# A fused recommender kernel: pair multiplies re-divided between DMA and TensorE, half of the DMAs issued by ScalarE, and folds put ahead of gathers

## The chip, the cores and the metric

One core of a Trainium2 chip. The metric is the device time of one execution in microseconds (us); lower is better. Engines are called PE (TensorE), DVE (VectorE), ACT (ScalarE), POOL (GpSimd) and SP (SyncE, which here only issues DMAs).

## The reference, cut to what matters

For 2048 examples, 26 fields of 32 numbers each are looked up in tables (`emb`). Two interaction layers ("CIN") and a dense network of three layers are computed from them and summed with a linear part.

```python
emb = tables[feat_idx, sparse]              # (2048, 26, 32)
x0 = xk = emb
for w, bb in ((conv1_w, conv1_b), (conv2_w, conv2_b)):
    hp = einsum('bhd,bmd->bhmd', xk, x0).reshape(-1, h * M, E)
    xn = sigmoid(einsum('oi,bid->bod', w, hp) + bb[None, :, None])
    xk, rest = xn[:, :half], xn[:, half:]    # rest is summed over E
deep = tanh(tanh(tanh(deep_x @ W1 + b1) @ W2 + b2) @ W3 + b3) @ deep_w
```

The second layer's product pairs the first layer's 64 results with each of the 26 fields. It is the bulk of the work, and the change is about it.

## The kernel before, in words

The 2048 examples are 16 tiles of 128, and each tile is four steps (`STEPS`) of 8 of the 32 numbers, so that a step has 8 x 128 = 1024 columns. After the 64 steps the dense network runs over all examples; the change does not touch it.

In a step the 26 fields are 13 pairs (n = 0 to 12, which fields by `ORDER`). For pair n, DVE multiplies a 128 x 1024 tile, in which each of two fields is repeated on 64 partitions, with `xk` (line 545), and PE contracts the product into `y2` (`contract`, line 627, four matmuls a pair). The repeated tile comes in one of two ways:

- for n in `BY_DMA` (nine pairs) SP reads it from `x0_rows`, a copy of the tile's embeddings in HBM, by two broadcast DMAs of 256 KB each, one for either half (`spread_by_dma`, line 377), into a buffer `xb` of its own. DVE multiplies in place, so the buffer is free for the next step when PE has contracted that pair.
- for n in `BY_PE` (6, 7, 11, 12) PE spreads it with four small matmuls for two pairs (`spread_pair`, line 603) into one of three PSUM slots `bc`; DVE reads PSUM and writes `hp`.

The first layer of the next step is computed beside this: PE fills three slots (uses K, line 614), ACT squares them (line 793), PE contracts them in two column halves (`contract_k`, line 621, "first 0" and "first 1") into the one PSUM bank `xn`, and ACT reads each half by three activations (`read_xn`, lines 797 to 799). PE waits for the read of the first half before it starts the second. Use T turns the embeddings for a later step (line 590) and ACT copies them (line 783). Use D, once a tile at the end of step 2, turns the next tile's embeddings for the dense network (line 599); ACT copies them to `deep_t` (lines 787, 789), and SP writes them to `x0_rows` (`dump`).

The order of PE's and ACT's work in a step is written out in `STEP_WORK`; each slot use takes the slot of the use three places before it (`slot_free`). Each engine runs its own list in order.

POOL gathers the embeddings of the next tile by 26 indirect DMAs (`gather`, line 432). It may begin when D has been turned (`free_emb`, line 459). Between gathers, in the places that `AHEAD` sets, it folds the sums of both layers (`add_up`, lines 447 to 452). When all 26 have landed, ACT makes the high part of the embeddings (`make_high`, line 780, in step 1 of a tile, right after its copy of T) and POOL the low part (line 439).

ACT may read the first layer's results for a new tile into `r1` (in step 3) only when POOL's last `r1` fold is done.

Of the kernel before, what the change touches and what calls it, by code (L numbers as in the profile page):

```python
# [14 lines left out]
P = 128  # L15
B, M, V, D, ND = 2048, 26, 1250, 32, 13
ROW = D + 1
# [6 lines left out]
H = 64  # L24
# [64 lines left out]
def is_t(use):  # L89
    return isinstance(use, tuple) and use[0] == "T"  # L90


# [27 lines left out]

AHEAD = 4, 10, 16
assert AHEAD[-1] <= M

# [13 lines left out]
def build(nc, table, sparse, dense_t, lin_dense, pair_a, pair_b, diag_a, diag_b, w2rows, conv1_b, conv2_b,  # L137
          cin_w, scalars, W1, b1, W2, b2, W3, b3, deep_w, select, ident_f, out):
    with ExitStack() as ctx:
# [95 lines left out]
        pool_held = sem("pool_held")  # L235
        sp_held = sem("sp_held")
        gathered = sem("gathered")
        high_made = sem("high_made")
# [51 lines left out]
        def product(n):  # L290
            return hp[BY_PE.index(n)] if n in BY_PE else xb[BY_DMA.index(n)]

        GATHERED = 16 * M
# [39 lines left out]
        def _(sp):  # L333
# [32 lines left out]
            def dump(t):  # L366
                sp.wait_ge(deep_copied, t + 1)
                hold()
                cols = bass.ds(t * P, P)
                sp.dma_start(x0_rows[bass.ds(t, 1), 0:(KD - 1) * P, :].rearrange("t (k p) b -> p (t k) b", p=P),  # L370
                             deep_t[:, 0:KD - 1, cols]).then_inc(dumped, 16)
                sp.dma_start(x0_rows[bass.ds(t, 1), (KD - 1) * P:M * ROW, :].rearrange("t p b -> p (t b)"),
                             deep_t[0:LAST_E, KD - 1, cols]).then_inc(dumped, 16)
                sp.wait_ge(dumped, t * (16 * DUMPS) + 16 * DUMPS)
                hold()

            def spread_by_dma(t, sl, i):
                for f in range(2):
                    first = (2 * ORDER[BY_DMA[i]] + f) * ROW + sl * STEP_D
                    row = x0_rows[bass.ds(t, 1), first:first + STEP_D, :].rearrange("t d b -> t (d b)")  # L380
                    sp.dma_start(xb[i][H * f:H * f + H, :], row.to_broadcast([H, COLS])).then_inc(spread[i], 16)

            def tile(t, is_first, ahead):
                for sl in range(STEPS):
                    s = t * STEPS + sl
                    for i, n in enumerate(BY_DMA):
                        if not (is_first and sl == 0):
                            sp.wait_ge(contracted, contracted_by(s - 1, n))
                            hold()
                        spread_by_dma(t, sl, i)  # L390
                if ahead > 0:
# [24 lines left out]
        def _(pool):  # L416
# [48 lines left out]
            free_emb(0, 3)  # L465
            gather(range(AHEAD[2]))

            def tile(t, is_first, ahead):
                if ahead > 0:
                    gather(range(AHEAD[2], M - 4))  # L470
                if not is_first:
# [113 lines left out]
        def _(pe):  # L585
# [8 lines left out]

            def turn_deep(slot):
                rows = emb[:, 0:M, :].rearrange("p m e -> p (m e)")
                for k in range(KD):
                    n = min(P, M * ROW - k * P)
                    last = nc.tensor.transpose(bc[slot][0:n, k * P:(k + 1) * P], rows[:, k * P:k * P + n], idf[:, :])  # L599
                last.then_inc(filled, 1)  # L600
# [31 lines left out]
            def slot_free(t, sl, use, is_first, ahead):  # L632
# [12 lines left out]
                else:  # L645
                    pe.wait_ge(deep_copied, t + 2)

            def fill(t, sl, use, ahead):
# [12 lines left out]
                else:  # L661
                    turn_deep(slot)

# [3 lines left out]
            turn_x0(1, 1)  # L667
            turn_deep(2)
            for k in range(K1):
                pe.wait_ge(x0t_copied, min(k + 1, 2))  # L670
                if k == 2:
                    pe.wait_ge(deep_copied, 1)
                spread_sum(k, k, x0t[0])
# [8 lines left out]
            def tile(t, is_first, ahead):  # L682
                for sl in range(STEPS):
# [30 lines left out]
                    if ("D", 0) in there:  # L714
                        slot_free(t, sl, ("D", 0), is_first, ahead)
                        fill(t, sl, ("D", 0), ahead)

# [49 lines left out]
        def _(act):  # L767
# [16 lines left out]

            def copy_deep(slot, t):
                cols = bass.ds(t * P, P)
                nc.scalar.activation(deep_t[:, 0:KD - 1, cols], bc[slot][:, 0:(KD - 1) * P].rearrange("p (k b) -> p k b", b=P),
                                     ACT.Copy)
                nc.scalar.activation(deep_t[0:LAST_E, KD - 1, cols], bc[slot][0:LAST_E, (KD - 1) * P:KD * P],
                                     ACT.Copy).then_inc(deep_copied, 1)  # L790
# [10 lines left out]
            def read_y2(s, sl):  # L801
                act.wait_ge(contracted, s * PAIRS + PAIRS)
                nc.scalar.activation(r2[:, sl, :], y2[:, :], ACT.Sigmoid, bias=bias2[:, :]).then_inc(y2_read, 1)  # L803

            act.wait_ge(pads_cleared, 2)
            make_high(0)
# [5 lines left out]
            act.wait_ge(w1_step, 7)  # L812
            copy_deep(2, 0)
            for k in range(K1):
                act.wait_ge(filled, 3 + k + 1)
                square(k, k)
            for c in range(2):
                act.wait_ge(k_contracted, c + 1)
                read_xn(0, 0, c)
            act.wait_ge(w2_loaded, W2_LOADED)  # L820

            def tile(t, is_first, ahead):
                for sl in range(STEPS):
# [3 lines left out]
                    for kind, what in STEP_WORK:  # L827
# [11 lines left out]
                        elif kind == "of_last" and not start:  # L839
                            if sl == 1 and not is_first:  # L840
                                act.wait_ge(r2_step, t * SUMS)
                            read_y2(s - 1, (sl - 1) % STEPS)
                        elif kind == "first" and ("K", 0) in there:
                            act.wait_ge(k_contracted, k_contracted_by(s, what))
                            if what == 0:
                                act.wait_ge(multiplied, s * PAIRS + 1)
                                if sl == STEPS - 1:
                                    act.wait_ge(r1_step, (t + 1) * SUMS)
                            read_xn((sl + 1) % 2, (sl + 1) % STEPS, what)
                    if ("D", 0) in there:  # L850
                        act.wait_ge(filled, filled_by(t, sl, ("D", 0), ahead))
                        copy_deep(slot_of(sl, ("D", 0), ahead), t + 1)

# [108 lines left out]
```

## Time and profile before

| | us |
|---|---|
| median of three runs | 1829.8 (1819.85 to 1834.06) |
| the profiled execution | 1826.01 |
| its span, first to last instruction | 1824.2 |
| start, up to the first contraction of pairs | about 79 |
| one tile (four steps), mean of 14, from D turned at 129.98 to D turned at 1433.43 | 93.1 |
| dense network and end, from about 1538 | 286 |

The page gives busy shares over the span of 87% for PE, 63% for DVE, 39% for ACT, 43% for POOL. The SP and ACT queues' DMAs share 16 DMA engines. Because the tiles repeat, one is best read by the order of events in it: a gain per tile counts 14 times.

### The profile page before, as it was taken

The page shows a single profiled execution, that of the slowest core. Times are in us where ns is not written, and L with a number is a line of the kernel's source. Part 1 is how long each engine was busy: PE and PEld are TensorE (multiplying, and loading weights), DVE is VectorE, ACT ScalarE, POOL GpSimd, SP SyncE. Part 2 cuts the span into 40 slices and gives each one's busy share as a digit, 9 for nine tenths or more (in the row PEclk, how much of TensorE's full clock was granted, in tenths as well). Part 3 has the DMA queues.
Part 4 walks back from the last instruction along what each step waited for, and adds up shares of the span by engine and source line. Part 5 has one row for each costly group of instructions (what it writes and reads, how often), then busy time and mean ns, then how long its engine had stood idle before and what let it go on. Part 6 is the DMA issues. An engine that isn't in the chain of part 4 may idle for free.

```text
span 1824.2 us, 23564 instructions
## 1 busy us (share of the span) xinstructions
PE 1586.2 (87%) x6584; PEld 690.7 (38%) x6584; DVE 1154.8 (63%) x992; ACT 704.1 (39%) x966; POOL 784.1 (43%) x631
## 2 busy tenths in 40 slices
PE   0799889969998979698989798899897997999998
PEld 0333333323333323233323232333232332887886
DVE  2376777656867766568676677677766777344442
ACT  1343434333343434234434343344343432445443
POOL 6728282637382735454545554455555112000000
PEclk9899999989999989898989898999998998999999
DMA  4799999979999989899999999899998996223231
GB/s 85 167 235 209 223 211 228 214 176 212 231 219 213 220 192 214 182 208 225 209 219 210 215 215 218 204 214 218 230 216 203 215 235 157 88 92 99 92 98 47
DMA packets 132283, 344.73 MB, mean 189 GB/s; under 512 B 30131, under 2 KB 50899, under 8 KB 132183
## 3 DMA queue, kind: packets, MB, share of 16 engines
q1 hardware_dynamic: 118936, 337.23, 79.1%
q0 software_dynamic: 13312, 7.06, 3.1%
q8 instruction: 19, 0.31, 0.1%
q14 instruction: 16, 0.13, 0.0%
HBM read 337.14 MB, written 7.04 MB: 189 GB/s over the span
## 4 chain that ended last, share of the span: by engine, by line
PE 44%; POOL 29%; issue 13%; DMA 9%; ACT 3%; DVE 1%; POOLq 0%; SPq 0%; ACTq 0%; DVEq 0%
POOL emb L432 23%; PE y L627 16%; PE bc L740 14%; PE xn L621 10%; DMA emb<-table,idx_stage 7%; POOL r L447 3%; POOL r L450 2%; PE bc L607 1%; DMA xb<-x_rows 1%; POOL sum L452 1%; PE bc L614 1%; ACT halves L780 1%; PE bc L599 1%; PE bc L590 1%; ACT r L799 1%
## 5 line engine op out<-in xcount | busy, mean ns | idle before, releaser
L545 DVE TENSOR_TENSOR xb<-xb,xk 128x1024 f32<-128x1024 f32 x576 | 743.3, 1319 | 233.9 <-DMA xb<-x_rows 193.0
L432 POOL DMA_INDIRECT emb<-table,idx_stage x416 | 523.6, 1259 | 152.3 <-issue 137.9
L627 PE MATMUL y<-xb,w2s 128*64 128x512 f32 x2304 | 556.5, 609 | 4.9 <-ACT r L803 4.9
L621 PE MATMUL xn<-sq,w1s 128*128 128x512 f32 x768 | 400.9, 663 | 121.2 <-ACT r L799 111.4
L545 DVE TENSOR_TENSOR hp<-bc,xk 128x1024 f32<-128x1024 f32 x256 | 301.2, 1218 | 197.4 <-PE bc L607 191.6
L621 PEld LDWEIGHTS xn<-sq,w1s 128*128 128x128 f32 x768 | 148.9, 208 | 318.4 <-issue 187.5
L797 ACT ACTIVATE xk<-xn,bias 64x512 f32<-64x512 f32 x128 | 87.4, 683 | 447.7 <-PE xn L621 304.5
L627 PEld LDWEIGHTS y<-xb,w2s 128*64 128x64 f32 x2304 | 150.2, 138 | 285.6 <-issue 266.9
L447 POOL TENSOR_TENSOR r<-r 128x512 f32<-128x512 f32 x96 | 131.3, 1375 | 293.7 <-ACT r L803 269.6
L793 ACT ACTIVATE sq<-bc 128x1024 f32<-128x1024 f32 x192 | 183.0, 1027 | 170.9 <-PE bc L614 143.8
L627 PE MATMUL y<-hp,w2s 128*64 128x512 f32 x1024 | 242.5, 594 | 0.0
L627 PEld LDWEIGHTS y<-hp,w2s 128*64 128x64 f32 x1024 | 74.1, 138 | 149.5 <-issue 139.7
L577 DVE TENSOR_TENSOR h_lo<-h_raw,h_hi 128x512 fp32r<-128x512 f32 x48 | 33.3, 693 | 142.5 <-ACT h_hi L891 142.5
L439 POOL TENSOR_TENSOR halves<-emb,halves 128x448 fp32r<-128x448 f32 x32 | 57.5, 1818 | 121.0 <-ACT halves L780 121.0
L614 PE MATMUL bc<-x0t,sel 64*128 64x512 f32 x384 | 64.8, 442 | 41.2 <-DVE hp L545 21.3
L740 PE MATMUL bc<-x_hi,w_hi 128*128 128x512 f32 (+1 forms) x224 | 88.4, 395 | 8.4 <-DVE w_lo L560 8.4
L780 ACT ACTIVATE halves<-emb 128x448 fp32r<-128x448 f32 x32 | 31.0, 1016 | 151.8 <-DMA emb<-table,idx_stage 151.8
L803 ACT ACTIVATE r<-y,bias 128x512 f32<-128x512 f32 x64 | 44.1, 690 | 116.9 <-PE y L627 98.4
L799 ACT ACTIVATE r<-xn,bias 64x512 f32<-64x512 f32 x128 | 87.7, 685 | 3.3
L590 PE MATMUL bc<-idr,halves 128*128 128x128 f32 x256 | 43.4, 294 | 51.7 <-POOL halves L439 49.4
L798 ACT ACTIVATE xk<-xn,bias 64x512 f32<-64x512 f32 x128 | 87.4, 683 | 1.6
L740 PE MATMUL bc<-x_hi,w_lo 128*128 128x512 f32 (+1 forms) x224 | 87.9, 393 | 0.0
(63 smaller groups left out, 1052.5 us busy)
## 6 DMA issues: line engine op xcount, KB each, us to landing
xb<-x_rows SPq DMA_DIRECT2D x1152, 256.0 KB
w_raw<-W SPq DMA_DIRECT2D x32, 448.0 KB, 3.1
w_raw<-W SPq DMA_DIRECT2D x16, 512.0 KB, 3.2
emb<-table,idx_stage POOLq DMA_INDIRECT x416
x_rows<-deep_t SPq DMA_DIRECT2D x16, 384.0 KB
w_raw<-W SPq DMA_DIRECT2D x8, 256.0 KB, 2.6
hp<-select SPq DMA_DIRECT2D x2, 512.0 KB, 4.9
x_rows<-deep_t SPq DMA_DIRECT2D x16, 45.0 KB
```

Of the source, the lines that this page charges most:

```text
L432: nc.gpsimd.indirect_dma_start(out=emb[:, m, :], out_offset=None, in_=table, in_offset=bass.IndirectOffsetOnAxis(ap=idx_stage[:, m:m + 1], ...
L447: nc.gpsimd.tensor_tensor(r[:, 0, :], r[:, 0, :], r[:, sl, :], ALU.add).then_inc(step, 1)
L545: nc.vector.tensor_tensor(product(n)[:, :], x[:, :], xk[sl % 2][:, :], ALU.mult).then_inc(multiplied, 1)
L590: last = nc.tensor.matmul(bc[slot][:, q * P:(q + 1) * P], halves[:, d:d + 2, :, :, :].rearrange("p c g i m -> p (c g i m)"), idr[:, :], st ...
L614: last = nc.tensor.matmul(bc[slot][:, c * CHUNK:(c + 1) * CHUNK], sel[rows, PAIRS + k, :], x[rows, :], start=True, stop=True)
L621: last = nc.tensor.matmul(xn[:, :], w1s[:, k, :], sq[k][:, cols], start=(k == 0), stop=(k == K1 - 1))
L627: last = nc.tensor.matmul(y2[H * c:H * c + H, :], w2s[:, ORDER[n], :], src[:, c * CHUNK:(c + 1) * CHUNK], start=(n == 0), stop=(n == PAIRS ...
L740: last = nc.tensor.matmul(bc[a % 2][:, 0:CHUNK], w[a % 2][part, k, :], x[part, at, :], start=(k == 0 and i == 0), stop=(k == rows - 1 and ...
L793: nc.scalar.activation(sq[k][:, :], bc[slot][:, :], ACT.Square).then_inc(squared, 1)
L797: nc.scalar.activation(xk[slot][0:H, cols], xn[0:H, :], ACT.Sigmoid, bias=bias1[0:H, :])
L798: nc.scalar.activation(xk[slot][H:P, cols], xn[0:H, :], ACT.Sigmoid, bias=bias1[0:H, :]).then_inc(xk_made, 1)
L799: nc.scalar.activation(r1[H * c:H * c + H, sl, :], xn[H:P, :], ACT.Sigmoid, bias=bias1[H:P, :]).then_inc(xn_read, 1)
```

## The change

- Six pairs are spread by PE (2, 3, 5, 6, 8, 9), in three groups of two, and seven come by DMA (0, 1, 4, 7, 10, 11, 12). `ORDER` is a new permutation of the fields over these places.
- SP issues only the first half of each DMA pair. ACT issues the second: for 10, 11 and 12 right after `read_y2`, for 0, 1, 4 and 7 of the next step behind waits for the contraction of pairs 1, 4 and 7, after its second `read_xn`.
- D is turned in two fills, of four and three transposes, in two slots, copied by three activations, and `deep_copied` counts twice a tile.
- POOL's last `r1` fold comes before `free_emb`, so outside the gathers; the gathers lie 12, fold, 6, and in the next tile 4, fold, 4.

```diff
-ORDER = [1, 2, 3, 4, 5, 6, 0, 7, 8, 9, 10, 11, 12]
-BY_PE = (6, 7, 11, 12)
-ORDER[11], ORDER[4] = ORDER[4], ORDER[11]
+ORDER = [3, 10, 0, 7, 4, 1, 8, 11, 2, 9, 5, 12, 6]
+BY_PE = (2, 3, 5, 6, 8, 9)
...
     ("first", 0),
-    ("fill", (6, 7)),
-    ("of_this", (0, 1, 2, 3)),
+    ("fill", (2, 3)),
+    ("of_this", (0, 1)),
     ("first", 1),
-    ("fill", (11, 12)),
-    ("of_this", (4, 5, 6, 7, 8)),
+    ("fill", (5, 6)),
+    ("of_this", (2, 3, 4)),
+    ("fill", (8, 9)),
+    ("of_this", (5, 6, 7, 8)),
...
+DEEP_PARTS = range(0, 4), range(4, KD)
...
-        fills = fills + [("D", 0)]
+        fills = fills + [("D", 0), ("D", 1)]
...
-AHEAD = 4, 10, 16
+AHEAD = 12, 18
...
+        EARLY = ((1, (0, 1)), (4, (4,)), (7, (7,)))
+        LATE = (10, 11, 12)
...
-            def spread_by_dma(t, sl, i):
-                for f in range(2):
...
+            def spread_first(t, sl, i):
+                sp.dma_start(xb[i][0:H, :], copies(t, sl, i, 0)).then_inc(spread[i], 16)
...
-                if ahead > 1:
-                    free_emb(t + 1, filled_by(t, SL_DEEP, ("D", 0), ahead))
-                    gather(range(AHEAD[0]))
                 add_up(t, 3, r1, r1_step, xn_read, 2, sum1)
                 if ahead > 1:
-                    gather(range(AHEAD[0], AHEAD[1]))
+                    free_emb(t + 1, filled_by(t, SL_DEEP, ("D", 1), ahead))
+                    gather(range(AHEAD[0]))
                 add_up(t, 2, r2, r2_step, y2_read, 1, sum2)
                 if ahead > 1:
-                    gather(range(AHEAD[1], AHEAD[2]))
+                    gather(range(AHEAD[0], AHEAD[1]))
...
+            def spread_second(t, sl, n):
+                i = BY_DMA.index(n)
+                act.dma_start(xb[i][H:P, :], copies(t, sl, i, 1)).then_inc(spread[i], 16)
...
+            act.wait_ge(dumped, 16 * DUMPS)
+            hold()
+            for n in BY_DMA:
+                spread_second(0, 0, n)
...
                             read_y2(s - 1, (sl - 1) % STEPS)
+                            for n in LATE:
+                                spread_second(t, sl, n)
...
+                    if not (ahead == 0 and sl == STEPS - 1):
+                        if sl == STEPS - 1:
+                            act.wait_ge(dumped, t * (16 * DUMPS) + 2 * 16 * DUMPS)
+                            hold()
+                        for by, ns in EARLY:
+                            act.wait_ge(contracted, contracted_by(s, by))
+                            hold()
+                            for n in ns:
+                                spread_second(t + (sl + 1) // STEPS, (sl + 1) % STEPS, n)
```

## Rows read from the trace of the kernel before

**Rows 1.** Windows: busy us of each engine, TensorE's granted clock, DMA share, GB/s

```profile
131.20:1433.40 1302.20, 1144.77 (x4683) 410.11 (x4683) 906.91 (x743) 495.15 (x672) 690.28 (x548) 0.94 0.94 213
```

**Rows 2.** Waits of the whole span: us in total, times, longest

```profile
DVE xb L545 <- DMA xb<-x_rows: 193.0, 201, 3.3
...
ACT halves L780 <- DMA emb<-table,idx_stage: 151.8, 16, 30.2
...
PE xn L621 <- ACT r L799: 111.4, 21, 13.3
...
ACT xk L797 <- POOL sum L452: 71.2, 14, 9.8
```

**Rows 3.** Timeline of POOL in one tile: start, us, then idle before and releaser

```profile
881.68 0.23 POOL L426 COPY idx_stage<-idx_all 128x26 int32 x1 [12.87 <-PE bc L599]
...
890.21 1.28 POOL L447 TENSOR_TENSOR r<-r 128x512 f32<-128x512 f32 x1
...
893.14 2.01 POOL L432 DMA_INDIRECT emb<-table,idx_stage  x1 [0.21 <-issue]
...
930.93 0.95 POOL L432 DMA_INDIRECT emb<-table,idx_stage  x1 [0.30 <-issue]
```

**Rows 4.** Timeline of ACT in step 1 of that tile

```profile
928.28 0.69 ACT L803 ACTIVATE r<-y,bias 128x512 f32<-128x512 f32 x1 [1.20 <-PE y L627]
928.86 0.59 ACT L783 ACTIVATE x0t<-bc 128x512 fp32r<-128x512 f32 x1
939.01 1.93 ACT L780 ACTIVATE halves<-emb 128x448 fp32r<-128x448 f32 x2 [9.56 <-DMA emb<-table,idx_stage]
```

**Rows 5.** Timeline of PE in that tile

```profile
880.34 0.98 PE L599 MATMUL bc<-idf,emb 128*128 128x128 f32 x7
882.48 0.98 PE L614 MATMUL bc<-x0t,sel 64*128 64x512 f32 x6 [1.15 <-ACT deep_t L789]
...
902.76 0.96 PE L614 MATMUL bc<-x0t,sel 64*128 64x512 f32 x6
...
923.68 0.96 PE L614 MATMUL bc<-x0t,sel 64*128 64x512 f32 x6 [1.49 <-DVE hp L545]
...
928.66 2.79 PE L621 MATMUL xn<-sq,w1s 128*128 128x512 f32 x6
931.38 0.51 PE L607 MATMUL bc<-x0t,sel 32*128 32x512 f32 x4
931.82 3.65 PE L627 MATMUL y<-xb,w2s 128*64 128x512 f32 x16
942.97 5.49 PE L621 MATMUL xn<-sq,w1s 128*128 128x512 f32 x6 [7.50 <-ACT r L799]
```

**Rows 6.** Windows in another tile's wait for its gathers, columns as in rows 1

```profile
752.00:754.00 2.00, 0.00 (x0) 0.00 (x0) 0.00 (x0) 0.00 (x0) 0.00 (x0) 0.50 1.01 219
...
760.00:765.00 5.00, 4.58 (x6) 1.79 (x6) 0.00 (x0) 0.37 (x1) 1.57 (x2) 0.58 0.00 0
```

**Rows 7.** Timeline of the first tile's last gather and of ACT's make_high behind it

```profile
41.44 0.95 POOL L432 DMA_INDIRECT emb<-table,idx_stage  x1 [0.30 <-issue]
...
44.56 1.90 ACT L780 ACTIVATE halves<-emb 128x448 fp32r<-128x448 f32 x2 [30.19 <-DMA emb<-table,idx_stage]
```

**Rows 8.** SP's issue of a spread DMA: ns min/median/max

```profile
L381 SPq DMA_DIRECT2D xb<-x_rows x1152: 3/468/1715, 57.2 to 1519.9; - x192
L381 SPq FUSED_REGOPS  x936: 2/37/897, 146.7 to 1345.5; - x188
```

**Rows 9.** DVE's multiplies by source: ns min/median/max

```profile
L545 DVE TENSOR_TENSOR xb<-xb,xk x576: 1207/1222/3025, 69.4 to 1530.9; 128x1024 f32<-128x1024 f32 x192
L545 DVE TENSOR_TENSOR hp<-bc,xk x256: 1206/1216/1226, 78.8 to 1533.2; 128x1024 f32<-128x1024 f32 x128
```

**Rows 10.** Groups of instructions: POOL's gathers, busy us and mean ns

```profile
L432 POOL DMA_INDIRECT emb<-table,idx_stage x416 | 523.6, 1259 | 152.3 <-issue 137.9 <-POOL idx_stage L426 13.2 <-ACT r L803 0.3
```

More of the change, by code:

```diff
@@ L90, in is_t, with is_d @@
     return isinstance(use, tuple) and use[0] == "T"
+def is_d(use):
+    return isinstance(use, tuple) and use[0] == "D"
 def is_product(use):
@@ L236, in build @@
         sp_held = sem("sp_held")
+        act_held = sem("act_held")
         gathered = sem("gathered")
@@ L291, in product, with copies @@
             return hp[BY_PE.index(n)] if n in BY_PE else xb[BY_DMA.index(n)]
+        def copies(t, sl, i, f):
+            first = (2 * ORDER[BY_DMA[i]] + f) * ROW + sl * STEP_D
+            row = x0_rows[bass.ds(t, 1), first:first + STEP_D, :].rearrange("t d b -> t (d b)")
+            return row.to_broadcast([H, COLS])
+        EARLY = ((1, (0, 1)), (4, (4,)), (7, (7,)))
+        LATE = (10, 11, 12)
+        assert sorted(n for by, ns in EARLY for n in ns) + list(LATE) == list(BY_DMA)
         GATHERED = 16 * M
@@ L366, in dump @@
             def dump(t):
-                sp.wait_ge(deep_copied, t + 1)
+                sp.wait_ge(deep_copied, t * 2 + 2)
                 hold()
@@ L465, in _ @@
             free_emb(0, 3)
-            gather(range(AHEAD[2]))
+            gather(range(AHEAD[1]))
             def tile(t, is_first, ahead):
                 if ahead > 0:
-                    gather(range(AHEAD[2], M - 4))
+                    gather(range(AHEAD[1], M - 4))
                 if not is_first:
@@ L593, in turn_x0, with turn_deep @@
                 last.then_inc(filled, 1)
-            def turn_deep(slot):
+            def turn_deep(slot, ks):
                 rows = emb[:, 0:M, :].rearrange("p m e -> p (m e)")
-                for k in range(KD):
+                for at, k in enumerate(ks):
                     n = min(P, M * ROW - k * P)
-                    last = nc.tensor.transpose(bc[slot][0:n, k * P:(k + 1) * P], rows[:, k * P:k * P + n], idf[:, :])
+                    last = nc.tensor.transpose(bc[slot][0:n, at * P:(at + 1) * P], rows[:, k * P:k * P + n], idf[:, :])
                 last.then_inc(filled, 1)
@@ L661, in fill @@
                 else:
-                    turn_deep(slot)
+                    turn_deep(slot, DEEP_PARTS[use[1]])
             pe.wait_ge(sel_rounded, 3)
@@ L667, in _ @@
             turn_x0(1, 1)
-            turn_deep(2)
+            turn_deep(2, range(KD))
             for k in range(K1):
@@ L713, in tile @@
                             contract(n)
-                    if ("D", 0) in there:
-                        slot_free(t, sl, ("D", 0), is_first, ahead)
-                        fill(t, sl, ("D", 0), ahead)
+                    for use in there:
+                        if is_d(use):
+                            slot_free(t, sl, use, is_first, ahead)
+                            fill(t, sl, use, ahead)
             over_tiles(pe, tile)
@@ L783, in copy_x0, with copy_deep, copy_deep_last @@
                 nc.scalar.activation(x0t[sl][:, :], bc[slot][:, 0:CHUNK], ACT.Copy).then_inc(x0t_copied, 1)
-            def copy_deep(slot, t):
+            def copy_deep(slot, t, ks, at):
                 cols = bass.ds(t * P, P)
-                nc.scalar.activation(deep_t[:, 0:KD - 1, cols], bc[slot][:, 0:(KD - 1) * P].rearrange("p (k b) -> p k b", b=P),
-                                     ACT.Copy)
-                nc.scalar.activation(deep_t[0:LAST_E, KD - 1, cols], bc[slot][0:LAST_E, (KD - 1) * P:KD * P],
+                src = bc[slot][:, at * P:(at + len(ks)) * P].rearrange("p (k b) -> p k b", b=P)
+                return nc.scalar.activation(deep_t[:, ks[0]:ks[-1] + 1, cols], src, ACT.Copy)
+            def copy_deep_last(slot, t, at):
+                cols = bass.ds(t * P, P)
+                nc.scalar.activation(deep_t[0:LAST_E, KD - 1, cols], bc[slot][0:LAST_E, at * P:(at + 1) * P],
                                      ACT.Copy).then_inc(deep_copied, 1)
@@ L812, in _ @@
             act.wait_ge(w1_step, 7)
-            copy_deep(2, 0)
+            copy_deep(2, 0, range(KD - 1), 0).then_inc(deep_copied, 1)
+            copy_deep_last(2, 0, KD - 1)
             for k in range(K1):
```

16 lines of the change are left out of this document (9 added, 7 removed).

## The prediction

> **What bounds the kernel now.** I read the windows first. Over the 14 repeating tiles PE is busy 1144.8 of 1302.2 us, the DMA engines 0.94 of the time, DVE and POOL far less [rows 1]. Two resources are near full, so the question is what each tile's idle time of PE waits for. PE's timeline of one tile gives the pace without waits: step 0 runs from the K fills at 902.76 to those at 923.68, 20.92 us with a wait of 1.49, so 19.43; turning D and waiting for its copy takes from 880.34 to 882.48, 2.14 [rows 5]. A tile of PE's own work is 4 x 19.43 + 2.14 = 79.9 us, and a tile takes 93.1 (1303.45 / 14, the table of times). So 13.2 us a tile is stall and slow clock.
>
> The waits name the places [rows 2]. PE's largest is on ACT's read of xn, 111.4 us in 21 times, up to 13.3. ACT in turn waits 151.8 us for gathers and 71.2 us for POOL's fold. DVE waits 193.0 us for spread DMAs, in bits of up to 3.3; by itself that costs PE only the small waits such as the 1.49.
>
> The timelines show how these join. POOL stages the indices at 881.68, when D is turned, and its last gather ends at 931.88 [rows 3]. ACT begins the high part at 939.01 after idling 9.56 us [rows 4]. PE, whose second contraction of K needs the read that ACT makes after that, starts at 942.97 after 7.50 us of nothing, and takes 5.49 us for six matmuls that took 2.79 with no such stop before them [rows 5]. That the DMA engines are full while PE stands still is seen in another tile: a share of 1.01 at 752 to 754 with PE idle and its clock at 0.50 (1.2 GHz), then a share of 0.00 at 760 to 765 [rows 6]. The last gather lands with the end of the backlog. From its issue to ACT's start is 7.1 us here [rows 3, 4] against 2.2 us in the first tile, ahead of all spreads [rows 7]. So a tile is a loop: stage, gathers, landing, high part, the rest of step 1, step 2, D, stage; and the DMA load stretches it.
>
> **The change part by part.**
>
> *Nine DMA pairs to seven.* 72 DMAs of 256 KB a tile are 18.9 MB, 95% of what 213 GB/s moves in 93.1 us. The DMA engines are busy 0.94 x 93.1 = 87.5 us a tile [rows 1]; with 56 of 72 spreads this is 87.5 x (1 - 0.95 x 16/72) = 69.0 us. Spreads no longer bound anything on the average, and DVE's waits for them and PE's waits behind these should nearly go.
>
> *Six PE pairs.* Two more pairs are four more spread matmuls, 0.44 us (931.38 to 931.82) [rows 5]. A step becomes 19.87. The slots cost little: fills 5 and 6 come right after the second contraction, and from there DVE has five multiplies (5 to 9) of 1.22 [rows 9], 6.1 us, before the next K fills need slot 9. PE meanwhile does seven pairs at 3.65/4 = 0.9 (the four pairs from 931.82) and another fill, 6.8 us [rows 5]. DVE has 0.7 us to spare.
>
> *Only two pairs between the two contractions of K.* These are 0.44 + 1.8 us after the first one's end, where there were four pairs. ACT's read takes three activations of about 0.69, 2.1. PE waits about 0.1 us a step for it: 20.0 us.
>
> *ACT issues seven DMAs a step.* SP's issue takes 0.468, with address arithmetic about 0.53 [rows 8]; I take this for ACT. Four of the seven lie behind waits at the end of a step where ACT has nothing else; the three late ones lie between the read of y2 and the copy of T, ahead of the read of xn. In the row, ACT ends its copy at 929.45; 1.6 later is 931.05, and the first contraction of K ends at 931.45 [rows 4, 5]. They just fit. In step 1 the high part (1.93) stands there too, so the second contraction starts 3.96 after the high part's start (939.01 to 942.97) [rows 4, 5], at 931.05 + 3.96 = 935.0, where PE was ready at 931.82 + 1.8 = 933.6: 1.4 us. What is queued behind a late issue on ACT is T's copy and the read, which PE waits for. Bounds: nothing, if they fit, to 1.715 each, SP's longest (a rival, below).
>
> *D in two slots.* The seven transposes are the same and the second copy is shorter than the one before; I leave 2.14 a tile.
>
> PE's own tile is now 4 x 19.87 + 3 x 0.1 + 1.4 + 2.14 = 83.3 us.
>
> *Folds ahead of gathers.* The last r1 fold sits between gathers from 890.21 to 893.14; less the usual gap of 0.30 it is 2.65 us of the loop [rows 3]. Ahead of the staging it lies beside PE's step 2, where the second contraction of K, two fills and seven pairs take 10.0 us and ACT's read of xn is done after 4.9 of them, so it is hidden. ACT's 71.2 us of waits for it go too, but I count nothing more for them: 14 stops like the one of 7.50 already make 105 of PE's 111.4 us [rows 2, 5].
>
> *Gathers beside fewer SBUF multiplies.* A gather takes 1.26 on the mean [rows 10] and 0.95 undisturbed [rows 3]; a multiply that reads SBUF can take 3.0, one that reads PSUM never over 1.23 [rows 9]. The two engines disturb each other in the first kind only, and that falls from 9 to 7 of 13. An excess of 0.31 x 2/9 x 26 gathers = 1.8 us of the loop; bounds 0 and 8 (all of the excess).
>
> *The loop.* Stage to high part was 939.01 - 881.68 = 57.3 us [rows 3, 4]. Less 2.65 and 1.8 it is 52.9 with a landing of 7.1, and 48.0 with one of 2.2. PE's own pace puts the high part at 0.8 (stage to K fills) + 2 x 20.0 + 7.4 (K fills at 923.68 to 931.05) = 48.2 after the stage. With the DMA engines at some 80% I take a landing of 4: 49.8, so PE loses 1.6 us more, 84.9 a tile. Together with the 1.4 this is a stop of 3.0 us. After the 7.50 us one the six matmuls lost 2.7 us to the clock, and after the one of 1.49 the fills lost nothing [rows 5]; I take half of 2.7. A tile is 86.2 us.
>
> *Start and end.* ACT issues seven DMAs before its first squares: 7 x 0.53 = 3.7, of which I count 3. The last five steps wait for nothing of this and grow by 0.57 each: 3.
>
> **Sum.** 1826 - 14 x (93.1 - 86.2) + 3 + 3 = 1735 us, against the profiled execution's own 1826.0 (its span 1824.2). The median of the runs is 1829.8, 4 above, inside their spread of 14; I add 2 of it and say **1737**. From the bounds: PE's pace undisturbed, 83.3, gives 1695; landing still 7.1 with the whole clock loss, 83.3 + 4.7 + 2.7 = 90.7, gives 1798.
>
> Two rules of the Trainium skill speak against parts of this. "DMA: Bandwidth & Descriptors", in the section on queues, rings and completion order, says that each DMA engine takes turns between the queues that have work; with ACT's queue beside SP's a gather would get a third of the turns in place of a half, so a backlog would hold it longer. No row here shows three queues; the lag of 7.1 with two is shown. By this rule the gather rival below is likelier than I make it. "Perfetto Trace Analysis", in its section on the HWDGE instruction, says that the descriptor generator is locked by one sequencer at a time; by it ACT's late issues could take SP's time besides their own, 1.06 each, and a step would lose 1.2 us (about 1800 in all).
>
> **Rivals.**
>
> *PE alone sets the pace* (chance 0.2): the gathers land ahead of need. For it: 48.0 of the loop against 48.2. Against it: the landing of 2.2 was seen with no spreads about [rows 7], and a share of 0.8 is not that. 83.3 a tile gives about 1697.
>
> *The gathers still set the tile* (0.2): the spreads come in bursts, six halves together at each step's start, just where the last gather lands, and the lag stays at 7. 90.7 a tile gives about 1800.
>
> *DVE becomes the bound* (0.08): between fills 5 and 9 and the K fills it has 0.7 us to spare. If POOL's folds stretch its multiplies, by up to 1.8 each [rows 9], PE waits, say 0.7 us more in each step: 2.8 x 14 = 39, about 1776.
>
> *ACT's issues come out slower than before* (0.07): the three late issues are on PE's path from (931.45 - 929.45) / 3 = 0.67 us each. To eat the whole gain they must cost 0.67 + (93.1 - 86.2) / 12 = 1.25 us each. At SP's longest, 1.715, a step loses 3.1 and a tile 12.5, so that a tile takes some 98 and the kernel 1826 + 14 x 5 + 6 = about 1905. For it: ACT's instructions stand in one line with them, and SP's issues are seen to stretch. Against it: the median of 0.468 over 1152 issues, even with the DMA engines full.
>
> *It doesn't do what it says*: only that the moved fold does not leave the loop, since POOL would wait in it for ACT; that is 2.65 us inside the range.
>
> **How the numbers follow.** The forecast has 0.45, the rivals 0.2, 0.2, 0.08, 0.07. The range 1695 to 1800 takes in all but the last and the tails. A measurement of this kernel tells about 1% (18 us) from no change. Slower by over that has ACT's rival, 0.06; within it 0.04, from the tail of the gathers' rival and small issues' cost; faster 0.9.
>
> **What would show it.** Right: a DMA share of about 0.8 in the repeating tiles; D to D about 86 us; ACT's wait for gathers at the high part down from over 9 us to some 2; no wait of ACT for POOL's fold; DVE's waits for spreads under 50 us in all; PE's K fills 20.0 us apart in steps 0, 2, 3. ACT's DMA issue at about 0.5 us. Wrong: PE's waits on ACT's read in every step (issues dear), on DVE's products at the K fills (DVE bound), or a stage to high part still over 52 us (the gathers' loop).

## The result, and the profile after

The median is 1766.34 us (four runs, 1753.84 to 1775.65) against 1825.66 for the kernel before (four runs): a ratio of 0.967, 95% interval 0.962 to 0.973. The profiled execution took 1775.65, its span 1773.5. It is faster, as forecast, and 29 us slower than the forecast of 1737. It is also not the whole result: when the same kernel was run again among the experiments it took 1937 and 1913 us, slower than the kernel before. The first profile is read here, the others with the experiments.

Windows over the 14 repeating tiles, D turned at 133.20 to D turned at 1386.60, columns as in rows 1:

```profile
133.20:1386.60 1253.40, 1157.50 (x4916) 411.10 (x4914) 861.13 (x743) 500.24 (x686) 662.22 (x546) 0.97 0.77 174
```

The DMA share fell from 0.94 to 0.77 [rows 1], and a tile from 93.1 to 1253.4 / 14 = 89.5 us. The waits of the whole span:

```profile
ACT halves L795 <- DMA emb<-table,idx_stage: 93.1, 13, 28.9
...
PE xn L635 <- ACT r L817: 85.2, 16, 10.4
...
DVE xb L559 <- DMA xb<-x_rows: 28.9, 4, 26.6
...
ACT r L821 <- POOL sum L468: 3.9, 1, 3.9
```

DVE's wait for spreads is gone but for the first (26.6 of 28.9 us; it was 193.0). ACT's wait for POOL's r1 fold (71.2) has no row left [rows 2]; the 3.9 shown are one wait for the r2 fold. What stayed is the wait for the last gather, and behind it PE's for the read of xn: 13 and 16 times, nearly once a tile. One tile shows them. PE:

```profile
847.78 0.98 PE L613 MATMUL bc<-idf,emb 128*128 128x128 f32 x7
849.70 0.96 PE L628 MATMUL bc<-x0t,sel 64*128 64x512 f32 x6 [0.94 <-ACT deep_t L807]
...
869.75 0.96 PE L628 MATMUL bc<-x0t,sel 64*128 64x512 f32 x6
...
889.73 0.97 PE L628 MATMUL bc<-x0t,sel 64*128 64x512 f32 x6
...
905.73 5.49 PE L635 MATMUL xn<-sq,w1s 128*128 128x512 f32 x6 [5.92 <-ACT r L817]
```

POOL's staging and last gather, and ACT's high part:

```profile
849.12 0.78 POOL L442 COPY idx_stage<-idx_all 128x26 int32 x1 [2.58 <-PE bc L613]
...
894.09 1.97 POOL L448 DMA_INDIRECT emb<-table,idx_stage  x1 [0.30 <-issue]
```

```profile
894.46 1.80 ACTq L829 DMA_DIRECT2D xb<-x_rows  x3
...
901.82 1.89 ACT L795 ACTIVATE halves<-emb 128x448 fp32r<-128x448 f32 x2 [4.85 <-DMA emb<-table,idx_stage]
```

K fills lie 20.05 and 19.98 apart, with no wait. From the staging to the end of the last gather (894.09 + 1.97) is 46.9 us, and ACT starts the high part 5.8 after that, 52.7 after the staging; it was 57.3 in the tile of [rows 3, 4]. 52.7 is also the mean of the 14 repeating tiles. ACT has by then issued its three late DMAs, in 1.80 us, and waited 4.85 for the gather. PE stops for 5.92, where it was 7.50, and its next six matmuls again take 5.49 [rows 5].

### The profile page after: what moved, and what is told of

Read it like the earlier page. It is cut to its first block, busy times and chain, and to the rows that moved or that the text cites. A ratio compares the mean times of both kernels' runs of the same rounds, so it can differ in the third digit from the quotient of the medians.

```text
span 1773.5 us, 23872 instructions
## 1 busy us (share of the span) xinstructions
PE 1600.1 (90%) x6840; PEld 690.3 (39%) x6840; DVE 1107.0 (62%) x992; ACT 708.9 (40%) x981; POOL 747.9 (42%) x631
## 4 chain that ended last, share of the span: by engine, by line
PE 53%; POOL 24%; issue 10%; DMA 6%; ACT 4%; DVE 2%; ACTq 1%; POOLq 0%; DVEq 0%
PE y L641 21%; POOL emb L448 21%; PE bc L755 15%; PE xn L635 12%; DMA emb<-table,idx_stage 5%; PE bc L621 2%; POOL r L463 2%; PE bc L628 1%; ACT halves L795 1%; POOL r L466 1%; PE bc L604 1%; PE bc L613 1%; DVE xb L559 1%; DVE hp L559 1%; ACT r L817 1%
## 5 line engine op out<-in xcount | busy, mean ns | idle before, releaser
L559 DVE TENSOR_TENSOR hp<-bc,xk 128x1024 f32<-128x1024 f32 x384 | 452.6, 1216 | 428.1 <-PE bc L621 428.1
L559 DVE TENSOR_TENSOR xb<-xb,xk 128x1024 f32<-128x1024 f32 x448 | 551.1, 1274 | 29.0 <-DMA xb<-x_rows 28.9
L448 POOL DMA_INDIRECT emb<-table,idx_stage x416 | 503.3, 1210 | 146.9 <-issue 133.1
L641 PE MATMUL y<-xb,w2s 128*64 128x512 f32 x1792 | 432.7, 596 | 0.8 <-ACT r L821 0.3
L641 PE MATMUL y<-hp,w2s 128*64 128x512 f32 x1536 | 382.7, 605 | 0.1
L641 PEld LDWEIGHTS y<-xb,w2s 128*64 128x64 f32 x1792 | 122.1, 137 | 238.4 <-issue 203.8
L641 PEld LDWEIGHTS y<-hp,w2s 128*64 128x64 f32 x1536 | 93.1, 136 | 165.8 <-issue 148.0
L621 PE MATMUL bc<-x0t,sel 32*128 32x512 f32 x768 | 97.6, 498 | 0.0
L621 PEld LDWEIGHTS bc<-x0t,sel 32*128 32x128 f32 x768 | 36.9, 182 | 152.2 <-issue 100.2
L755 PE MATMUL bc<-x_lo,w_hi 128*128 128x512 f32 (+1 forms) x224 | 87.7, 391 | 0.0
```

The source lines that it names most:

```text
L448: nc.gpsimd.indirect_dma_start(out=emb[:, m, :], out_offset=None, in_=table, in_offset=bass.IndirectOffsetOnAxis(ap=idx_stage[:, m:m + 1], ...
L559: nc.vector.tensor_tensor(product(n)[:, :], x[:, :], xk[sl % 2][:, :], ALU.mult).then_inc(multiplied, 1)
L621: last = nc.tensor.matmul(bc[slot][:, c * CHUNK:(c + 1) * CHUNK], sel[rows, ORDER[n], :], x[rows, :], start=True, stop=True)
L641: last = nc.tensor.matmul(y2[H * c:H * c + H, :], w2s[:, ORDER[n], :], src[:, c * CHUNK:(c + 1) * CHUNK], start=(n == 0), stop=(n == PAIRS ...
L755: last = nc.tensor.matmul(bc[a % 2][:, 0:CHUNK], w[a % 2][part, k, :], x[part, at, :], start=(k == 0 and i == 0), stop=(k == rows - 1 and ...
```

## The experiments

Twelve runs, two of them of the changed kernel itself, were made in four sets, and each set has its own runs of the kernel before. The kernel under study is "the changed kernel"; unedited, it is the control of the second and third set. These two sets ran on one chip, the first and fourth on two others.

**First set: the parts of the change** (kernel before 1822.2).

*The fold alone, in the kernel before.*

```diff
                 add_up(t, 2, r1, r1_step, xn_read, 2, sum1)
-                if ahead > 1:
-                    free_emb(t + 1, filled_by(t, SL_DEEP, ("D", 0), ahead))
-                    gather(range(AHEAD[0]))
                 add_up(t, 3, r1, r1_step, xn_read, 2, sum1)
                 if ahead > 1:
-                    gather(range(AHEAD[0], AHEAD[1]))
+                    free_emb(t + 1, filled_by(t, SL_DEEP, ("D", 0), ahead))
+                    gather(range(AHEAD[1]))
```

> The kernel before with one part of the change alone: POOL's last r1 fold ahead of the staging, gathers 16, 6, 4 with the r2 folds as before. If the tile is the loop of stage, 26 gathers, landing, high part (my theory), the fold's 2.65 us leave it: the tile goes from 93.1 to 90.4 and the kernel to about 1826 - 37 = 1789. Rival: the spread DMAs bound the tile beside it (87.5 us of DMA work a tile), the landing comes with the end of the backlog however early the gathers were issued: under 15 us gained, 1811 to 1826.

Measured: 1783.5, ratio 0.977 (0.972 to 0.983), 90.7 us a tile. That is near the 1789 of the loop theory and far from the rival's 1811 or more. A fold of 2.65 us that leaves the loop brings 93.1 - 90.7 = 2.4 us a tile, so the tile of the kernel before is set by this loop. Moving POOL's fold alone brings 2.3%, where the whole change brought 3.3% in its first measurement.

*The changed kernel with the fold back between the gathers.*

```diff
-                add_up(t, 3, r1, r1_step, xn_read, 2, sum1)
                 if ahead > 1:
                     free_emb(t + 1, filled_by(t, SL_DEEP, ("D", 1), ahead))
-                    gather(range(AHEAD[0]))
+                    gather(range(4))
+                add_up(t, 3, r1, r1_step, xn_read, 2, sum1)
+                if ahead > 1:
+                    gather(range(4, AHEAD[0]))
```

> The kernel after with the last r1 fold back between the gathers (4, fold, 8, fold, 6, and 4, fold, 4). The loop theory: 2.65 us a tile lost again, 89.5 to 92.2, the kernel about 37 us over after's 1766, 1803. Rival: POOL has slack now that PE and the DMAs set the tile: within 8 us of 1766.

Measured: 1862.4, ratio 1.024 (1.018 to 1.031), 94.9 us a tile. Far too slow for the fold.

*The changed kernel with all spreads issued by SP.*

```diff
             def spread_first(t, sl, i):
-                sp.dma_start(xb[i][0:H, :], copies(t, sl, i, 0)).then_inc(spread[i], 16)
+                for f in range(2):
+                    sp.dma_start(xb[i][H * f:H * f + H, :], copies(t, sl, i, f)).then_inc(spread[i], 16)
...
-                            for n in LATE:
-                                spread_second(t, sl, n)
...
-                            for n in ns:
-                                spread_second(t + (sl + 1) // STEPS, (sl + 1) % STEPS, n)
```

> The kernel after with all DMAs of the spreads issued by SP, none by ACT. Theory: the landing of the last gather (5.7 us) depends on how many spreads are queued with it, not on the queue they came from; ACT's early high part is hidden behind the gathers: within 12 us of 1766, the start 3 us shorter. Rival by turns between three queues: the landing falls by 2 to 3 us with one queue fewer, and the kernel gains 28 to 42 us, about 1730.

Measured: 1830.8, ratio 1.003 (0.998 to 1.007), 92.2 us a tile.

*The changed kernel with 22 gathers a tile.* It leaves out the lookups of the last four fields and has zeros in their place.

```diff
-        GATHERED = 16 * M
+        GATHERED = 16 * (M - 4)
...
-            nc.gpsimd.memset(emb[:, M:2 * PER_GROUP, :], 0.0).then_inc(pads_cleared, 1)
+            nc.gpsimd.memset(emb[:, M - 4:2 * PER_GROUP, :], 0.0).then_inc(pads_cleared, 1)
...
-                    gather(range(M - 4, M))
+                    gather(range(M - 6, M - 4))
```

> The kernel after with 22 gathers a tile in place of 26; the last four fields' embeddings are left at zero, so this work is left out. Theory: four gathers are some 6 us of the loop, the high part could begin at about 46.7 after the staging, ahead of the 48.2 at which PE needs it, so PE's own pace is left, 83.3 a tile: 14 x 6.2 = 87 us gained over after, about 1680. Rival: PE's stop in step 1 is ACT's own (its late issues and the high part) or DVE's: less than 30 us gained, over 1736.

Measured: 1885.0, ratio 1.031 (1.022 to 1.038), 97.9 us a tile. Less work, and 119 us more than the first measurement of the changed kernel. No theory on record allowed that. Its waits show a releaser that the first profile of the changed kernel does not have at all:

```profile
ACT xk L815 <- remote: 205.5, 14, 19.5
DVE hp L559 <- remote: 177.1, 21, 17.4
```

"remote" is a wait whose end the profile can put down to no instruction. In the kernel before it is one row:

```profile
ACT xk L797 <- remote: 41.8, 6, 9.3
```

All such rows together are 41.8 us in the kernel before, and 137.3, 276.5 and 391.6 us in the last three kernels. So the set did not say what the parts are worth, and the changed kernel itself had to be run as a control.

**Second set: the control, and where the late issues stand** (kernel before 1816.2).

*The changed kernel again, unedited.*

> The changed kernel itself, unaltered, as a control: the three variants of it so far (folds back, one queue, 22 gathers) came out 64 to 119 us above the 1766 of the changed kernel, and their traces show ACT and DVE waking up to 19 us after PE's last record of what they wait for, which the changed kernel's trace does not. Theory: this is a matter of how the gathers lie against the other engines' work in each program, so the control is 1766 within 15 and shows no such waits. Rival: it is a matter of the chip, then the control is at 1800 or over and shows them too.

Measured: 1937.5 (1935.8 to 1942.0), ratio 1.069 (1.061 to 1.076). So it is not a matter of each program, as the first theory had it: the same program gives both. Windows over its 14 tiles, D at 138.90 to D at 1553.20, and its waits:

```profile
138.90:1553.20 1414.30, 1185.92 (x4916) 409.88 (x4914) 870.66 (x743) 499.48 (x686) 589.01 (x546) 0.92 0.67 154
```

```profile
ACT xk L815 <- remote: 213.1, 14, 21.6
DVE hp L559 <- remote: 170.4, 22, 18.9
...
ACT halves L795 <- DMA emb<-table,idx_stage: 30.1, 1, 30.1
...
PE xn L635 <- ACT r L817: 15.9, 16, 1.1
```

A tile is 101.0 us. The wait at the high part is gone (the 30.1 is the first tile's) and so is PE's behind it: nothing in the tile waits for gathers any more. In their place stands one long stop a tile, soon after the staging. In its timelines of PE, ACT, DVE and POOL:

```profile
846.04 2.84 PE L635 MATMUL xn<-sq,w1s 128*128 128x512 f32 x6
848.81 0.50 PE L621 MATMUL bc<-x0t,sel 32*128 32x512 f32 x4
...
871.11 0.80 PE L621 MATMUL bc<-x0t,sel 32*128 32x512 f32 x4 [19.04 <-DVE hp L559]
```

```profile
867.62 0.68 ACT L815 ACTIVATE xk<-xn,bias 64x512 f32<-64x512 f32 x1 [21.64 <-remote]
```

```profile
869.83 2.35 DVE L559 TENSOR_TENSOR hp<-bc,xk 128x1024 f32<-128x1024 f32 x2 [18.89 <-remote]
```

```profile
835.36 0.79 POOL L442 COPY idx_stage<-idx_all 128x26 int32 x1 [2.58 <-PE bc L613]
...
854.45 0.96 POOL L448 DMA_INDIRECT emb<-table,idx_stage  x1 [0.16 <-issue]
...
865.70 0.94 POOL L448 DMA_INDIRECT emb<-table,idx_stage  x1 [0.30 <-issue]
```

ACT waits for a contraction that PE ended at 848.88, and DVE for a fill that PE ended at 849.31. They start only at 867.62 and 869.83, 18.7 and 20.5 us later. PE then stops for their products. POOL meanwhile issues gather after gather, 0.94 each with 0.30 between, and ACT wakes 1.0 us after the last of these.

The trace also records when a semaphore changes (the counter by which one engine tells another that it is done), which the views above leave out. PE's update for ACT is recorded at 867.60, 0.02 us before ACT starts, and its updates for five fills and contractions between 869.72 and 869.94. So ACT and DVE did not sleep on: the signal that they wait for came late. In this trace 128 of PE's updates are recorded more than 1 us after the last instruction of PE that makes them, and none of ACT's, DVE's or POOL's; no wait of PE is "remote". The first profile has no such update of PE, the kernel before 35. Two limits hold: the ends of matmuls are modelled, so their results may have been late with their signals, and many updates are missing from these records.

SP is late too. Its two dump DMAs in the changed kernel's first profile, and in this one:

```profile
765.83 0.49 SPq L388 DMA_DIRECT2D x_rows<-deep_t  x1
766.55 0.38 SPq L390 DMA_DIRECT2D x_rows<-deep_t  x1
```

```profile
842.49 0.96 SPq L388 DMA_DIRECT2D x_rows<-deep_t  x1
844.88 1.40 SPq L390 DMA_DIRECT2D x_rows<-deep_t  x1
856.22 21.60 SPq L397 DMA_DIRECT2D xb<-x_rows  x4
```

The first begins 7.1 us after the staging for 6.2, and the second issue took 1.40 us where it had taken 0.38; that is its longest, the median of the 16 is 0.70. The four after them spread over 21.60, but each of these waits for a contraction by PE. PE's timeline from the staging to its second contraction of K is the first profile's: contraction 10.10 us after the K fills (760.18 and 770.28 there, 835.94 and 846.04 here). One kernel, then, with two behaviours that part some 7 us after the staging.

Not every stop lasts to the end of the gathers. In another tile ACT wakes between two of them:

```profile
455.31 0.68 ACT L815 ACTIVATE xk<-xn,bias 64x512 f32<-64x512 f32 x1 [13.81 <-remote]
```

```profile
454.38 0.94 POOL L448 DMA_INDIRECT emb<-table,idx_stage  x1 [0.30 <-issue]
455.63 0.94 POOL L448 DMA_INDIRECT emb<-table,idx_stage  x1 [0.30 <-issue]
```

Of the 28 such stops of over 5 us in this trace 14 end so, with a gather going on or the next one following at once.

*The three late issues behind ACT's read of xn.* In `STEP_WORK`'s loop they move from after `read_y2` to after the first `read_xn`:

```diff
                             read_y2(s - 1, (sl - 1) % STEPS)
-                            for n in LATE:
-                                spread_second(t, sl, n)
...
                             read_xn((sl + 1) % 2, (sl + 1) % STEPS, what)
+                            if what == 0 and not start:
+                                for n in LATE:
+                                    spread_second(t, sl, n)
```

> The kernel after with ACT's three late issues moved from behind the read of y2 to behind its first read of xn. The loop theory: half of the burst of six spreads that meets the last gather goes, the landing falls from 5.7 to about 3.5 us and ACT copies T 1.6 us earlier: the tile from 89.5 to about 87, the kernel about 1766 - 35 = 1731. Rival (landing independent of the burst): within 10 us of the control. Second rival: as in the variants so far, ACT and DVE wake late, over 1800.

Measured: 1873.4, ratio 1.032 (1.024 to 1.041), 64 us below the control; over 1800, as the second rival had it.

*The same, and in step 1 the late spreads held until the gathers have landed.*

```diff
+                        if sl == 1 and ahead > 0 and n == LATE[0]:
+                            sp.wait_ge(gathered, t * GATHERED + 2 * GATHERED)
+                            hold()
                         spread_first(t, sl, i)
```

> The same, and in step 1 SP holds its first halves for pairs 10, 11 and 12 until all gathers have landed, so that no spread is queued with the last gathers. The loop theory: the landing falls to about 2.5 us, the high part begins 49.4 after the staging, PE's stop shrinks to 2 us and the clock stays up: the tile about 84, the kernel about 1766 - 75 = 1691. Rival (landing independent of the burst): no better than the run before. Second rival: late wake-ups, over 1800.

Measured: 1858.5, ratio 1.026 (1.017 to 1.034). That is 79 below the control, but only 15 of it by the hold, whose interval overlaps the other's. Both kernels still have the stops with no releaser (129.3 and 119.1 us of ACT's, longest 10.1, against 213.1 and 21.6), and in neither does ACT wait at the high part behind the first tile, so they do not test the theory of the landing.

*The r2 fold behind all gathers*, so that they run with one pause fewer:

```diff
-                    gather(range(AHEAD[1], M - 4))
+                    gather(range(AHEAD[1], M))
                 if not is_first:
                     add_up(t - 1, STEPS - 1, r2, r2_step, y2_read, 1, sum2)
-                if ahead > 0:
-                    gather(range(M - 4, M))
```

> The kernel after with POOL's r2 fold of step 3 behind the last gather in place of ahead of the last four. The loop theory: three instructions, some 4.4 us, leave the way to the last gather, ACT's read of y2 in step 1 waits some 1.5 us for them: the tile from 89.5 to about 86.5, the kernel about 1766 - 40 = 1726. Rival: a pause in the gathers is what keeps the other engines' wake-ups short; without it they come late, and the kernel is slower than the control by over 30 us, as with 22 gathers.

Measured: 1996.8, ratio 1.102 (1.093 to 1.111), 104.6 us a tile and stops of up to 23.0 us. With one pause fewer it is worse by 59 us, as the rival wanted, which points at the gathers.

**Third set: pauses between the gathers** (kernel before 1830.1).

*The changed kernel a third time.*

> The changed kernel once more, unaltered. It was 1766 first and 1937 in the first control. If it has two states that hold for a whole set of runs, it comes out near one of the two, and its trace shows SP's late issues and ACT's and DVE's late wake-ups in the second alone. Rival: the time is spread anywhere between, so that no single figure stands for it.

Measured: 1912.8 (1907.9 to 1925.2), ratio 1.055 (1.043 to 1.067), with 323.5 us of remote waits.

*The gathers tied to PE's progress.* Every fourth gather waits until PE has contracted the pairs that it should have by then:

```diff
-            def gather(fields):
+            def gather(fields, t, tied=True):
                 for m in fields:
+                    if tied and m > 4 and m % 4 == 0:
+                        pool.wait_ge(contracted, contracted_by((t - 2) * STEPS + SL_DEEP, 8 + m - 4))
+                        hold()
```

> The kernel after with gathers 8, 12, 16, 20 and 24 of a tile tied to PE's contractions (each waits for a count that PE reaches some 3 to 10 us earlier when it does not stand still), so that POOL stops soon after PE stops. Theory: gathers that go on are what keeps the other engines' wake-ups late, since in the control DVE and ACT wake when POOL comes to a wait: the stop in step 3 shrinks from up to 19 us to under 8, and in the slow state the kernel comes out at least 80 us below the control of this call. Rival: the gathers have no part in it, POOL's extra waits only put the gathers later: the same as the control, or above it by 10 to 100 us. Where the control is in the good state, both theories want it within 20 us of it.

Measured: 1790.4 (1784.7 to 1794.9), ratio 0.985 (0.974 to 0.995), 122 below the control of its set. Nothing was taken out; waits were added. ACT's and DVE's remote waits fell from 323.5 to 204.1 us, the longest from 18.0 to 9.6:

```profile
ACT xk L818 <- remote: 123.6, 14, 9.6
DVE hp L562 <- remote: 80.5, 23, 9.1
```

A stop now looks like this, in the timelines of POOL and of ACT, DVE and PE:

```profile
789.45 0.95 POOL L451 DMA_INDIRECT emb<-table,idx_stage  x1 [0.30 <-issue]
790.41 1.27 POOL L466 TENSOR_TENSOR r<-r 128x512 f32<-128x512 f32 x1
...
793.54 0.97 POOL L451 DMA_INDIRECT emb<-table,idx_stage  x1 [1.85 <-remote]
```

```profile
792.56 0.68 ACT L818 ACTIVATE xk<-xn,bias 64x512 f32<-64x512 f32 x1 [9.59 <-remote]
```

```profile
792.69 2.36 DVE L562 TENSOR_TENSOR hp<-bc,xk 128x1024 f32<-128x1024 f32 x2 [5.62 <-remote]
```

```profile
793.97 0.64 PE L624 MATMUL bc<-x0t,sel 32*128 32x512 f32 x4 [4.95 <-DVE hp L562]
```

ACT and DVE wake 2.2 and 2.3 us after the last gather before the pause (789.45 + 0.95), not at the end of all of them, and PE loses 4.95 in place of 19.04. Of the 18 stops of over 5 us in this trace 15 end in a pause, 1.8 to 3.3 us after a gather; in the control of this set 22 of 31 ended with gathers going on. Whether a pause of a fixed length would do as well as a wait for PE was not tried.

**Fourth set: the ties with the other edits, and closer ties** (kernel before 1823.3).

*Ties by four, with the moved late issues and the hold*: the three edits above together.

> The tied gathers together with ACT's late issues behind its first read of xn and SP's first halves of pairs 10 to 12 held in step 1 until the gathers have landed (both as in the earlier run). Over the third run of the changed kernel the ties gave 122 us and left stops of 4 to 5 us in step 3; without ties, late and held issues gave 79 us over the control. If the two are separate (late wake-ups in step 3; gathers' landing and ACT's order in step 1), the gain over the tied kernel's 1790 is what the tied kernel still loses in step 1, some 1 to 2 us a tile: 1765 to 1780. Rival: both gains came from the same stop, or the hold costs DVE its data: 1785 or over.

Measured: 1768.7 (1766.0 to 1770.7), ratio 0.970 (0.965 to 0.975), 88.4 us a tile, as expected.

*The same with a tie at every second gather.*

```diff
-                    if tied and m > 4 and m % 4 == 0:
+                    if tied and m > 4 and m % 2 == 0:
```

> The same with a tie at every second gather from 6 in place of every fourth from 8. Theory: a stop of PE ends as soon as POOL comes to a wait, and with ties twice as close it comes 2.5 us earlier on the mean: 2 us a tile less, 25 to 35 us below the run beside it. Rival: the added waits lengthen the gathers' loop (13 waits of some 0.2 us) by as much as they save: within 10 us of the run beside it.

Measured: 1753.5 (1749.9 to 1758.4), ratio 0.961 (0.957 to 0.965), 87.5 us a tile: 15 below ties by four, short of the 25 to 35 of the theory and more than the rival's 10. Its waits:

```profile
ACT xk L821 <- remote: 99.4, 15, 11.3
...
DVE hp L565 <- remote: 39.6, 10, 16.2
...
ACT halves L801 <- DMA emb<-table,idx_stage: 32.9, 2, 30.1
```

The stops are shorter in sum (141.9 us of ACT's and DVE's, for 226.2 with ties by four) and not gone, and at the high part ACT waits for gathers in two places only, one of them the first tile's 30.1. It is the fastest kernel of the study, 3.9% below the kernel before on the same chip. Whether it also beats the changed kernel where that takes 1766 was not measured, since the two never ran in one set.

## Why the prediction was right and where it was not

**The first measurement, by the steps.** Right: the DMA share (0.77 for 0.8); DVE's waits for spreads (28.9 for under 50); K fills 20.0 us apart, so the rival in which DVE becomes the bound falls; ACT's issue (448 of them, median 0.492, three in 1.80 for the 1.6 counted), so the rival of dear issues falls too; the r1 fold out of the loop, shown by itself at 2.4 us a tile for 2.65, in a kernel with more remote waits than the one it is compared with. The start grew by 3.2 for 3 (D at 133.20, was 129.98).

Two terms of the tile were mis-sized. *The landing* was taken as 4 between bounds of 2.2 and 7.1; it measured 5.8. With 46.9 us from staging to the last gather's end, for 45.8 forecast, the high part comes at 52.7, not 49.8: 2.9 us. About half of the missing 1.1 is *the gathers' conflict with DVE*: a gather's mean went from 1259 ns [rows 10] to 1210, or 1.3 us a tile, for the 1.8 counted. *The clock* was taken at half of 2.7; PE's stop was twice as long as forecast and the six matmuls paid in full (5.49 for 2.79): 1.35. In the tile shown, the longer stop (5.92 for 3.0) and the clock make 4.3. Turning D gave 0.2 back (849.70 - 847.78 = 1.92 for 2.14), and the tiles differ, with the high part from 47.7 to 57.2 after the staging; the mean tile took 89.5 for 86.2, 3.3 more. The sum closes: 1735 + 14 x 3.3 + 0 at the start - 7 at the end is 1774, and the profiled execution took 1775.65. The 7 is the end, from the last D, which became 3.9 shorter and was forecast 3 longer. Of the forecast and the rivals, the tile lies nearest to the rival in which the gathers still set it (90.7), and its mark for wrong, a high part later than 52 after the staging, is met. Its reason, spreads in bursts around the last gather, was not tested: in the kernels that move or hold the late spreads nothing waited for the last gather. So the mechanism of the forecast held at this measurement, with the landing, between its bounds, taken too small. That the measurement fell there is in part luck: it is the only one of the three of this kernel in which the effect told below is missing.

The landing fell from 7.1 to 5.8, less than the backlog did. The Trainium skill's "DMA: Bandwidth & Descriptors" (the section on queues, rings and completion order) has each DMA engine take turns between the queues with work, so that a gather gets a third of the turns in place of a half and its landing should stay long. A landing that fell less than the load does not speak against it, but the kernel with one queue had other stops, so no run here tells the rule from a mere size. The steps stayed at 20.0 us. "Perfetto Trace Analysis" in the Trainium skill (the section on the HWDGE instruction) has the descriptor generator locked for one sequencer at a time, from which the prediction estimated a loss of 1.2 a step. This trace does not agree: 248 of ACT's 448 issues overlap one of SP's in time, and they took 0.498 us in the median, the others 0.492; SP's took 0.469 and 0.468.

**What the forecast did not have.** The largest effect is in no term, bound or rival: in the two later sets the changed kernel lost 171 and 146 us against its first measurement (1937.5 and 1912.8 for 1766.3), while the kernel before stayed between 1816 and 1830 in every set. There its verdict turns round, 5 to 7% slower. Every step took for granted that PE's signal reaches the engine that waits as PE's instructions end; that is what failed.

What the runs show of it:

- The loss is in the stops that no instruction ends: 405.8 us of ACT's and DVE's waits in the control, none in the first profile. A tile of 101.0 less 89.5, times 14, is 161 of the 171 us.
- The late signals are PE's. None of ACT's, DVE's or POOL's is recorded over 1 us late in any run, and POOL has such waits only in the tied kernels, where it waits for PE (22.5 and 18.2 us with ties by four).
- It depends on how POOL's gathers follow each other. The same instructions with pauses took 122 us less; with one pause fewer, 59 us more. In the tied kernel most stops end within some 3 us of a pause. In the two controls 14 of 28 and 22 of 31 end while gathers go on, so a pause brings the end forward and is not needed for it.
- The stops fell where the late issues were moved (ACT's longest from 21.6 to 10.1), so where ACT stands when the gathers run matters as well.
- It is not tied to one chip: every kernel with the change had such waits in all four sets, on three chips, and only the first measurement had none. The changed order gives POOL twelve gathers in a row right behind the staging, where the kernel before had four, then the fold. The kernel before with the fold ahead has ten, and more such waits than unedited (122.1 us for 41.8).

What stays open: what PE's signals need that a run of gathers holds; why the first measurement of the changed kernel had none of it; and whether the level goes with the chip or with something else that changed between the sets, since the control ran on one chip alone. The records of semaphore updates leave a rival: of the 6656 that the gathers' landings make, the first profile holds 6516, the control 1850 and the slowest kernel 1302. So it may be that recording them has a part in it, and no run tells. With that the first set can't price the parts: the kernels with the fold back and with one queue had 79.7 and 122.4 us of such waits on DVE, and no control beside them.

## What to carry to other kernels

Run the unedited kernel again in each set in which its parts are taken off: here only the control showed that the change has two levels, 3% faster and 5 to 7% slower, and that most of the first set measured something else. A wait whose releaser the profile does not know is a mark to ask whose signal it is, and what another engine issues without a pause at that time: here it was always PE's, and POOL's gathers. An engine with time to spare that issues many indirect DMAs may be better paced by the progress of the engine that sets the time: here the added waits gained 122 us over a control of 1913; beside a changed kernel that takes 1766 they were not tried.

## What the hardware showed that was not expected

- While POOL issued gathers back to back, PE's semaphore updates were recorded up to 20 us after the instructions that make them (20.7 in the control), and ACT and DVE started with them; no update of ACT, DVE or POOL is recorded over 1 us late. An SP issue of 0.38 us became 1.40 at the beginning of one such stretch.
- Adding waits to an engine off the critical path took 6.4% off the time (1912.8 to 1790.4).
- In these traces the landing did not fall in proportion to the load: with the DMA share at 0.77 for 0.94 the last gather still took 5.8 us for 7.1, and 2.2 with no spreads about [rows 7].
- ACT issued a DMA in 0.49 us, SP in 0.47, also where the two overlapped, and ACT's reads stayed in time with three of its issues ahead (K fills 20.05 and 19.98 apart with no wait).
